# Attention weights made with the neighbour on the partitions, x loaded transposed, high products first

## The reference

```python
# layer 0, per graph:  x [128, 512], A [128, 128] of 0/1 with ones on the diagonal
h     = relu(layernorm(x))
feats = einsum('nf,hfu->hnu', h, W0)                     # 512 -> 8 heads x 64
e_self, e_neigh = feats . a_self, feats . a_neigh        # [8, 128] each
logit = leaky_relu(e_self[:, :, None] + e_neigh[:, None, :], 0.2) + NEG_BIG * (1 - A)
x     = x + relu(softmax(logit, -1) @ feats + b0)
# layer 1:
h = relu(layernorm(x))
y = hgconv(h, adj, W1, b1)                               # 512 -> 1024
y = layernorm(relu(y)) * gamma + beta
x = x + (h + hgconv(y, adj, W2, b2))                     # 1024 -> 512
# hgconv(x) = D^-1 H B^-1 H^T (x @ W^T) + b, with H = (adj != 0)
```

## Time and profile before

| | |
|---|---|
| median of 3 runs | 2611.56 us |
| the profiled execution | 2612.08 us |
| its span, first to last instruction | 2610.3 us |
| busy: PE, PEld, DVE, ACT, POOL | 2559.5, 2245.7, 1880.3, 1518.2, 1458.9 us |
| mean granted clock of PE | 0.995 of full speed |
| DMA: moved, share of 16 engines' time | 158.4 MB, 18.0% |

### The profile page before, as it was taken

How to read it: one execution, slowest core, us unless ns; L and a number is a source line. 1 busy time by engine, 2 the same in 40 slices (tenths; PEclk the granted TensorE clock), 3 DMA queues, 4 the chain that set the end, 5 groups by cost and what they waited for, 6 DMA issues and landing times.

```text
span 2610.3 us, 51365 instructions
## 1 busy us (share of the span) xinstructions
PE 2559.5 (98%) x15508; PEld 2245.7 (86%) x15508; DVE 1880.3 (72%) x4638; ACT 1518.2 (58%) x3593; POOL 1458.9 (56%) x2196
## 2 busy tenths in 40 slices
PE   4999999999999999999999999999999999999998
PEld 3888888888888888888888888888888888888886
DVE  6777777777777777777777777777777777777774
ACT  3565556556555555656655565565565555556553
POOL 5555555555555555555555555555555555555553
PEclk8999999999999999999999999999999999999999
DMA  4111111111111111111111111111111111111110
GB/s 151 52 55 62 58 60 63 58 60 55 66 60 55 63 58 60 62 59 60 55 62 59 60 63 58 60 57 64 60 54 62 58 60 63 58 60 55 65 51 25
DMA packets 85593, 158.70 MB, mean 61 GB/s; under 512 B 16832, under 2 KB 33216, under 8 KB 85568
## 3 DMA queue, kind: packets, MB, share of 16 engines
q1 hardware_dynamic: 85568, 158.39, 18.0%
HBM read 124.26 MB, written 34.08 MB: 61 GB/s over the span
## 4 chain that ended last, share of the span: by engine, by line
PE 96%; DVE 1%; issue 0%; ACT 0%; POOL 0%; POOLq 0%; DVEq 0%
PE p_w1a L793 14%; PE p_w1a L795 14%; PE p_w1a L794 14%; PE p_att L864 8%; PE p_w1b L793 5%; PE p_w1b L794 5%; PE p_w1b L795 5%; PE p_w1b L898 4%; PE p_att L844 4%; PE p_ta L811 4%; PE p_fa L794 2%; PE p_fa L795 2%; PE p_fa L793 2%; PE p_fb L794 2%; PE p_fb L793 2%; PE p_fb L795 2%
## 5 line engine op out<-in xcount | busy, mean ns | idle before, releaser
L359 POOL TENSOR_TENSOR rs<-ve,halfpow 128x1 f32<-128x1 f32 x128 | 115.0, 898 | 550.6 <-DVE ve L745 550.6
L793 PE MATMUL p_w1a<-W_hi,rT_hi 128*128 128x512 f32 x1024 | 414.8, 405 | 0.0
L794 PE MATMUL p_w1a<-W_lo,rT_hi 128*128 128x512 f32 x1024 | 403.7, 394 | 0.0
L795 PE MATMUL p_w1a<-W_hi,rT_lo 128*128 128x512 f32 x1024 | 403.5, 394 | 0.0
L424 ACT ACTIVATE att<-u,shifts 128x128 f32<-128x128 f32 x1024 | 400.3, 391 | 4.7 <-DVE shifts L705 4.7
L425 ACT ACTIVATE att_low<-u,shifts 128x128 f32<-128x128 f32 x1024 | 400.2, 391 | 0.0
L349 POOL TENSOR_TENSOR u<-u,mask 128x1024 f32<-128x1024 f32 x128 | 307.2, 2400 | 29.2 <-POOL mask L346 17.4
L319 POOL TENSOR_TENSOR ve<-mv,eps 128x1 f32<-128x1 f32 x256 | 93.0, 363 | 411.3 <-DVE mv L630 326.1
L477 ACT ACTIVATE rT_hi<-p_tb 128x512 fp32r<-128x512 f32 x128 | 76.7, 599 | 330.0 <-PE p_tb L811 330.0
L760 DVE SCALAR_TENSOR_TENSOR z<-p_w1a,rs,t_bc 128x512 f32<-128x512 f32 x128 | 96.1, 750 | 218.3 <-PE p_w1a L795 218.3
L864 PE MATMUL p_att<-feats,attT 128*128 128x65 f32 x2048 | 242.5, 271 | 2.2 <-ACT attT L467 2.2
(11 more groups left out here) (127 smaller groups left out, 7128.5 us busy)
## 6 DMA issues: line engine op xcount, KB each, us to landing
u<-en_rows SPq DMA_DIRECT2D x128, 512.0 KB, 3.6
x_in<-in_x SPq DMA_DIRECT2D x128, 256.0 KB, 2.6
out<-raw SPq DMA_DIRECT2D x128, 256.0 KB, 2.1
adj_in<-in_adj SPq DMA_DIRECT2D x128, 128.0 KB, 2.4
en_rows<-eT SPq DMA_DIRECT2D x512, 1.0 KB
raw<-in_W1T SPq DMA_DIRECT2D x2, 1024.0 KB, 11.0
raw<-in_W2T SPq DMA_DIRECT2D x2, 1024.0 KB, 9.8
raw<-in_W0T SPq DMA_DIRECT2D x1, 1024.0 KB, 6.5
```

The source lines that it names most:

```text
L359: nc.gpsimd.tensor_tensor(rs1[:, :], ve1[:, :], halfpow[:, :], ALU.pow).then_inc(s_rs1, 1)
L793: mm(dst, hi, w_hi, start=first, stop=False)
L794: mm(dst, hi, w_lo, start=False, stop=False)
L795: return mm(dst, lo, w_hi, start=False, stop=final)
```

## The change

It changes three things.

1. **The attention's logits are made with the neighbour on the partition.** The upper bound of each node's logits is found as before from `u` (now with the mask's low form). Then, for each node and head, DVE computes two numbers (`ab`: the shift for slope 1 and for slope 0.2), transposes them in blocks, and SP sends them through DRAM to all partitions: `AB` [128, 2, 8, 128], with the node along the free axis. For each head ACT adds 0.2 e_neigh (a number for each partition) to the second half (L488), and DVE makes `logit = max(AB0 + e_neigh, AB1)` (`leaky`, L588). POOL adds the transposed mask to all heads at once (L403), and one ACT instruction makes all exponentials (L459). The result has the neighbour on the partition, and PE takes it as it is: the eight transposes and the copy are gone, and so are `larger` and the 16 exponentials.
2. **x is also loaded transposed** (`xT`, one more DMA of 256 KB for each graph). The mean of x goes as a ninth row with e_neigh of the graph before through DRAM (`en_mu`, L698; L298 to L303), POOL subtracts it (`xc`, L389), ACT and DVE split relu(x - mean) into `h0`. The factor 1/std is applied after the product, where the features leave PSUM (L602) and on the 16 extra columns (L687 to L689). The four transposes of xn are gone.
3. **High products first.** PE does the matmuls that need only the `_hi` part of an operand before those that need `_lo`, and waits for `_lo` only ahead of the latter. The product with W0 is no longer mixed from both halves: all 12 matmuls of `p_fa` come first, then `p_fb`.

Beside these the order inside a turn changes on POOL, DVE and ACT. Shortened to its core:

```diff
@@ SP, turn
+                if g.within(NG) and (g.loop is not None or g.base >= 2):
+                    load_xT(g)
                 g = t.plus(2)
                 if g.within(NG):
-                    sp.wait_ge(s_eT, g.count())
+                    sp.wait_ge(s_abT, g.count())
                     for q in range(4):
-                        sp.dma_start(en_rows[:, 32 * q:32 * (q + 1)], eT[32 * q:32 * q + HEADS, :]).then_inc(s_en_out, 16)
-                    sp.wait_ge(s_en_out, g.count(per=64))
-                    sp.dma_start(u[:, g.slot(2), :, :].rearrange("p h n -> p (h n)"), ...
+                        sp.dma_start(ab_rows[:, 32 * q:32 * (q + 1)], abT[32 * q:32 * q + 2 * HEADS, :]).then_inc(s_ab_out, 16)
+                    sp.wait_ge(s_ab_out, g.count(per=64))
+                    sp.dma_start(AB[:, :, :, :].rearrange("p a h n -> p (a h n)"), ...
...
+                g = t.plus(4)
+                if g.within(NG + 1):
+                    sp.wait_ge(s_en_muT, g.count())
+                    for q in range(4):
+                        sp.dma_start(en_rows[:, 32 * q:32 * (q + 1)], en_muT[32 * q:32 * q + HEADS + 1, :]).then_inc(s_en_out, 16)
+                    sp.wait_ge(s_en_out, g.count(per=64))
+                    sp.dma_start(u[:, :, :].rearrange("p h n -> p (h n)"), ...
@@ POOL, turn
-                    nc.gpsimd.tensor_tensor(mask[:, :], ones[:, :], adj_in[:, g.slot(4), 0, :], ALU.subtract).then_inc(s_absent, 1)
-                    nc.gpsimd.tensor_tensor(mask[:, :], mask[:, :], absent[:, :].broadcast_to([P, N]), ALU.mult).then_inc(s_mask, 1)
+                g = t.plus(4)
+                    nc.gpsimd.tensor_tensor(xc[:, :, :], xT_in[:, g.slot(2), :, :],
+                                            u[:, HEADS:HEADS + 1, :].broadcast_to([P, DC, N]), ALU.subtract).then_inc(s_xc, 1)
+                g = t.plus(3)
+                    nc.gpsimd.tensor_tensor(u[:, 0:HEADS, :], u[:, 0:HEADS, :],
+                                            mask_low[:, :].unsqueeze(1).broadcast_to([P, HEADS, N]), ALU.add).then_inc(s_u, 1)
+                g = t.plus(2)
+                    pool.wait_ge(s_leaky, g.count())
+                    nc.gpsimd.tensor_tensor(logit[:, :, :], logit[:, :, :],
+                                            maskT[:, :].unsqueeze(1).broadcast_to([P, HEADS, N]), ALU.add).then_inc(s_logit, 1)
@@ ACT, turn
-                for i in range(half * HH, (half + 1) * HH):
-                    nc.scalar.activation(att[:, i, :], u[:, g.slot(2), i, :], ACT.Exp, bias=shifts[:, 0, i:i + 1])
-                    last = nc.scalar.activation(att_low[:, i, :], u[:, g.slot(2), i, :], ACT.Exp, bias=shifts[:, 1, i:i + 1],
-                                                scale=SLOPE)
+                    nc.scalar.activation(attT[:, :, :], logit[:, :, :], ACT.Exp).then_inc(s_exp, 1)
...
+                    for i in range(HEADS):
+                        nc.scalar.activation(AB[:, 1, i, :], AB[:, 1, i, :], ACT.Identity,
+                                             bias=e[:, g.slot(2), 2, i:i + 1]).then_inc(s_low, 1)
@@ DVE
+            def leaky(g):
+                for i in range(HEADS):
+                    dve.wait_ge(s_low, g.count(per=HEADS) - HEADS + 1 + i)
+                    last = nc.vector.scalar_tensor_tensor(logit[:, i, :], AB[:, 0, i, :], e[:, g.slot(2), 0, i:i + 1],
+                                                          AB[:, 1, i, :], ALU.add, ALU.max)
+                last.then_inc(s_leaky, 1)
@@ PE, turn
-                    pe.wait_ge(s_hg_lo, g.count())
-                    hidden(g, 0, p_w1a)
-                    hidden(g, 1, p_w1b)
+                    pe.wait_ge(s_hg_hi, g.count())
+                    for c in range(DC):
+                        high(p_w1a[:, :], hg_hi[:, part(c)], W1_hi[:, c, 0:HALF], W1_lo[:, c, 0:HALF], c == 0)
+                    pe.wait_ge(s_hg_lo, g.count())
+                    for c in range(DC):
+                        last = low(p_w1a[:, :], hg_lo[:, part(c)], W1_hi[:, c, 0:HALF], c == DC - 1)
...
-                    for i in range(HEADS):
-                        last = nc.tensor.transpose(p_att[:, i * N:(i + 1) * N], att[:, i, :], ident[:, :])
...
-                    transposes(p_ta, xn, s_xnT)
```

More of the change, by code:

```diff
@@ L230, in load, with load_xT @@
                 sp.dma_start(adj_in[:, s, :, :], adj2[bass.ds(n, 1), :, :, :].rearrange("a p t n -> p (a t) n")).then_inc(s_in[s], 16)
+            def load_xT(g):
+                if g.has(2):
+                    sp.wait_ge(s_xc, g.count(2))
+                n = g.base if g.loop is None else g.loop * UNROLL + g.base
+                sp.dma_start(xT_in[:, g.slot(2), :, :],
+                             xT[bass.ds(n, 1), :, :, :].rearrange("a p c n -> p (a c) n")).then_inc(s_xT[g.slot(2)], 16)
             def load_piece(n):
@@ L360, in turn @@
                     shift(g, nm1, rs1, nb1, s_nm1, s_rs1, s_nb1)
+                g = t
+                if g.within(NG):
+                    if g.has(1):
+                        pool.wait_ge(s_z, g.count(1))
+                    rstd(g, mv2, ve2, rs2[:, :], s_mv2, s_ve2, s_rs2)
                 g = t.plus(2)
@@ L612, in turn @@
+                    dve.wait_ge(s_ab, g.count())
+                    if g.has(1):
+                        dve.wait_ge(s_ab_out, g.count(1, per=64))
+                    nc.vector.transpose(abT[:, :], ab[:, :]).then_inc(s_abT, 1)
                 g = t.plus(4)
@@ L633, in turn @@
+                g = t.plus(4)
+                if g.within(NG + 1):
+                    if g.within(NG):
+                        dve.wait_ge(s_mv0, g.count())
+                    if g.has(1):
+                        dve.wait_ge(s_en, g.count(1))
+                        dve.wait_ge(s_en_out, g.count(1, per=64))
+                        dve.wait_ge(s_xc, g.count(1))
+                    nc.vector.transpose(en_muT[:, :], en_mu[:, :]).then_inc(s_en_muT, 1)
                 g = t.plus(2)
@@ L877, in turn @@
                     transposes(p_tb, r[:, HALF:DH], s_rT)
-                    for c in range(HC):
-                        if c % CB == 0:
-                            if g.base == 0:
-                                pe.wait_ge(k_lo2, 1 + c // CB)
-                            pe.wait_ge(s_rT_lo, g.count(per=2) - 1 + c // CB)
-                        k = slice(c * P, (c + 1) * P)
-                        last = three(p_w1a[:, :], rT_hi[:, k], rT_lo[:, k], W2_hi[:, c, :], W2_lo[:, c, :], c == 0, c == HC - 1)
+                    for m in range(2):
+                        if g.base == 0:
+                            pe.wait_ge(k_lo2, 1 + m)
+                        pe.wait_ge(s_rT_hi, g.count(per=2) - 1 + m)
+                        for c in range(m * CB, (m + 1) * CB):
+                            high(p_w1a[:, :], rT_hi[:, part(c)], W2_hi[:, c, :], W2_lo[:, c, :], c == 0)
+                        pe.wait_ge(s_rT_lo, g.count(per=2) - 1 + m)
+                        for c in range(m * CB, (m + 1) * CB):
+                            last = low(p_w1a[:, :], rT_lo[:, part(c)], W2_hi[:, c, :], c == HC - 1)
                     last.then_inc(s_w2, 1)
@@ L888, in turn @@
                 if g.within(NG):
-                    features(2, 0)
+                    features(g, 1, range(2))
                 g = t.plus(1)
@@ L902, in turn @@
                 if g.within(NG):
-                    features(2, 1)
-                    features(3, 0)
-                    features(3, 1).then_inc(s_feats, 1)
+                    features(g, 1, range(2, DC)).then_inc(s_feats, 1)
                 g = t.plus(2)
```

435 lines of the change are left out of this document (208 added, 227 removed).

## The result

The changed kernel takes 3068.73 us (median of 4 runs, 3059.88 to 3071.04), the kernel before 2611.44 us beside it (2611.14 to 2611.99). The ratio is 1.1745, 95% interval 1.1731 to 1.1758: slower by 457 us. The forecast was 2970 us, with a range of 2680 to 3110. The profiled execution took 3059.88 us, its span is 3058.1 us, TensorE's mean granted clock 0.942.

What follows compares the result with a forecast made beforehand. PE was taken to bound the kernel before, at 19.80 us a turn. Its work of 18.58 plus waits of 2.4 and 1.5 gave 22.5, so 2612 + 345 + 15 = 2972 us, rounded to 2970; range 2680 to 3110.

Steps and rivals of the forecast that it cites:

- High products first: In W1 and W2: takes away only PE's waits for hg_lo, worth under 7.4 us in all.
- PE's work: In each turn on PE: transposes and change of kind go, 1.22 us less, leaving 18.58 us.
- Place 1: Ahead of z: leaky meets POOL's beT, xc and u, 3.4 us in sum; PE waits 2.4 us.
- Place 2: Ahead of r: neg_s meets z_lo, neg_m the first rest, 1.8 us in sum; PE waits 1.5 us.
- The turn: Loop turn of 18.58 + 2.4 + 1.5 = 22.5 us, 2.7 more than 19.80; chance 0.62.
- slips between: Ahead of r on DVE: ab, between neg_s and neg_m meeting POOL instructions, was given no meeting of its own.
- Start and end: Outside the loop: two DRAM round trips, W0 waiting for the transposed mean, less late POOL work: +15 us, bounds 0 and +40.
- AB and u: DMA transfers in a turn: AB at most 10 us, hidden; u 7 to 8 us, hidden or slightly short.
- The clock: Rival: PE's idle time lowers its clock, adding 1 to 2 us a turn; chance 0.13 together with a late AB.
- DVE's slack: Rival that PE stays the bound: slack of 0.7 us at place 1, 0.2 at place 2 absorbs meetings; chance 0.09.
- The signs: Profile after: PE busy near 83%, waits for z and r, chain mostly on DVE, L588 maximum above 2 us.
- The copy in the earlier trace: L553 copy of 32 columns on DVE, 2.58 us for two, ending with a POOL instruction: read as exclusion.

Runs made afterwards that it cites:

- both through PSUM: Changed kernel with the low half of the logits in PSUM, and the row maximum and tiny instructions behind it through PSUM: 2524.88 us, ratio 0.967 to the kernel before.
- the old order of products: Changed kernel with W1 and W2 again high, high, low per chunk, behind the waits for hg_lo and rT_lo: 3071.91 us.
- the experiment with more work: Kernel with both through PSUM, plus two unneeded DVE maxima a turn straight ahead of leaky: 2687.6 us.

## Why the prediction was right, point by point

**PE's work.** 1.22 us less in a turn, 18.58: right. The shortest turns with both through PSUM have 18.5 us.

**Place 1.** Forecast 3.4 us of meetings and a wait of 2.4 us for z; measured in the turn shown `leaky` at 5.51 us against 2.15 in PSUM, 3.4 more, and 2.39 us of waiting (2.27 on average). The fourth, the sixth and the seventh are the blocked ones, beside POOL's beT, xc and u, and they lose 0.2, 1.0 and 2.1 us, as said one by one:

```profile
1418.79 0.54 DVE L588 SCALAR_TENSOR_TENSOR logit<-AB,e 128x128 f32<-128x128 f32 x1
...
1419.52 1.36 DVE L588 SCALAR_TENSOR_TENSOR logit<-AB,e 128x128 f32<-128x128 f32 x1
1420.80 2.44 DVE L588 SCALAR_TENSOR_TENSOR logit<-AB,e 128x128 f32<-128x128 f32 x1
```

The pieces laid end to end gave 2.7 us of waiting; the 2.4 was a judgement, and that it fits so well is in part luck.

**Place 2.** Forecast 0.8 for neg_s, 1.0 for neg_m and 1.5 of waiting for r; measured 0.81, 1.05 and 1.32.

**The turn.** Forecast 22.5, mean 23.04, 0.54 over the forecast, or 69 us. The term that was mis-sized is place 2, where ab "slips between". By the prediction's own pieces it could as well have met POOL's second sum, which starts as neg_m ends. In the trace it is a matter of hundredths: 0.02 us ahead of that sum it takes 0.17, in the loop body's first turn, 0.06 behind it, 1.26. With ab out of POOL's reach (neg_m to PSUM) the turn is 22.42 against the forecast's 22.5.

The terms of the sum were also off in a way that hides in it. Over 2000 us of the loop PE is busy 1721.73 us, 20.0 us a turn and not 18.58, above all because the clock falls in 90 turns. The waits are shorter for it: 2.2 and 1.0 us a turn, not 2.4 and 1.5. Even in a turn with the full clock PE's busy time is 19.00; the first matmuls behind a wait are longer (0.47 instead of 0.39 us), which makes a small part of that, and the rest I can't place.

**Start and end.** Forecast +15 us, bounds 0 and +40. The first z comes at 125.0 instead of 90.3: +35, within the bounds and 20 us over the value. Half of it is there at PE's first product with W0, at 41.5 instead of 22.8, where the transposed mean was named as the cause: POOL's first xc waits 23.4 us for u. POOL's first low half of a weight starts at 35.18 instead of the earlier trace rows's 17.29, and beside it stand the round trips: `leaky`'s input waits 9.4 us for its transfer in the first turn. With the 69 us this makes up 89 of the 99 us between forecast and median; the profiled execution is itself 9 us under the median.

**AB and u.** Hidden, as forecast: they land after 4.9 and 4.2 us, against the earlier trace rows, and in the whole run ACT waits 17 us for AB. POOL waits 54 us for u, of which 38.5 are its first three waits, ahead of the loop.

**The clock** was priced as a rival at 1 to 2 us a turn, "part of it in DVE's shadow". All of it is in that shadow: it falls to half for some 3.4 us in 90 of the 127 turns, and keeping it up in most of them gained nothing. So the rival had the right event and the wrong price for this kernel; where DVE is shorter, the price was 1.5 us.

**How I put it.** The prediction added two waits to PE's turn. Its number is right, but the old order of products shows that it is DVE's turn that counts: a delay of PE is absorbed, while time that DVE isn't blocked comes back. Both countings come to the same number here, since DVE's 17.5 us plus 5.2 is where PE's 18.6 plus its waits is too. The first would have failed for an edit on PE. That DVE needed 17.5 us against PE's 18.6 is also why only some 1.1 of the 5.2 us could be absorbed: I had put DVE's slack at 0.7 and 0.2 us in the two places, and the experiment with more work gives 1.2 in a turn.

**The signs.** PE is busy 85% (forecast 83), `leaky` has a mean of 0.72 us and a maximum of 2.48, neg_s and neg_m have means of 1.00 and 1.09, all as listed. The chain that was to lie mostly on DVE can't be read: the profile follows it back only some 10 us from the end.

**The copy in the earlier trace rows.** I read it as an instance of two SBUF inputs, but it has one. So one input is no sure protection, and the kernel with both through PSUM shows it again, on an instruction that takes 0.17 us alone:

```profile
106.87 4.10 DVE L722 TENSOR_SCALAR cnt<-G 128x2 f32<-128x2 f32 x1
```

```profile
101.34 9.61 POOL L329 TENSOR_TENSOR W_lo<-raw,W_hi 128x2048 fp32r<-128x2048 f32 x2
```

It ends with POOL's second W_lo (110.95 us). The loop shows no such case, so it costs nothing there.

**High products first** does nothing in it, as said; that it would be worth 1.9 us a turn in a better version I did not see.

The Trainium skill, "SBUF — State Buffer", section "Who interferes with whom", says that a DVE instruction with two SBUF inputs and a GpSimd one that reads SBUF shut each other out for a whole instruction. This case agrees, both with the second SBUF input and without it: 1024 of 1024 `leaky` with one input in PSUM take 333 to 348 ns, where with two SBUF inputs they took up to 2480.

## What to carry to other kernels

When DVE gets near to PE's load, count its turn as own work plus blocked time: an instruction of 8 columns with two SBUF inputs costs what is left of POOL's instruction, here 1.0 to 1.2 us instead of 0.17. Before giving such an instruction to DVE, ask whether one of its inputs can stand in PSUM, where spare columns or a bank between two uses will do (for the instruction types moved here; `cnt` above was blocked with one SBUF input). Here two such moves turned a loss of 17.5% into a gain of 3.3%. An edit that takes away waits, such as the order of products, is worth no more than the waits that are there: nothing before, 248 us in the repaired version. So it is measured again when the bound has moved.
